# Adaptive-norm transformer block on one core: cosine product on VectorE from PSUM, second key and query projections at other places, 768-key tile transposed through VectorE and DMAs

## What is computed

```python
# x (2, 1024, 256), 16 heads of 128, all float32
h = layernorm(x) * (1 + ca) + sa                 # sa, ca, ... = silu(c) @ wmod
q = (h @ Wq + bq) * 128 ** -0.5;  k = h @ Wk + bk;  v = h @ Wv + bv      # per head
q, k = [t * cos(pos) + rotate_half(t) * sin(pos) for t in (q, k)]        # along the head's 128 columns
attn = softmax(causal(q @ k.T));  x = x + ga * ((attn @ v) @ Wo + bo)
h = layernorm(x) * (1 + cb) + sb
x = x + gb * ffn(h)                              # silu(gate) * up, down; 704 wide, integer weights
```

## Time and profile before

| | |
|---|---|
| median of 3 runs | 1030.65 us (1030.63 to 1032.5) |
| profiled execution, own time | 1031.39 us |
| its span | 1029.6 us |
| busy: TensorE matmuls | 970.8 us, 94% |
| VectorE | 784.1 us, 76% |
| ScalarE | 669.5 us, 65% |
| GpSimd | 764.7 us, 74% |
| DMA engines, mean | 39.2% |

### The profile page before, as it was taken

The page is one execution under the profiler, slowest core; times in us unless marked ns, Lnnn a source line. Parts: engine busy times, 40 slices in busy tenths (PEclk is TensorE's granted clock), DMA queues, the critical chain, the costliest instruction groups (busy, mean ns, idle before and its releaser), DMA issues.

```text
span 1029.6 us, 19698 instructions
## 1 busy us (share of the span) xinstructions
PE 970.8 (94%) x5853; PEld 854.3 (83%) x5853; DVE 784.1 (76%) x1605; ACT 669.5 (65%) x1385; POOL 764.7 (74%) x532
## 2 busy tenths in 40 slices
PE   6988999999999999999999999999999999998897
PEld 5877888888888888888888888888888788887787
DVE  6857877777788788877787778877887777877644
ACT  5756656676666666666666666666666567767763
POOL 3487877788778877787778878787778777885653
PEclk9999999999999999999999999999999999999999
DMA  7524443343334433443434333543344335431011
GB/s 248 166 79 139 118 118 101 107 131 114 102 101 139 127 113 111 138 127 100 115 97 141 103 111 97 148 127 107 107 142 124 109 99 159 139 103 42 1 42 42
DMA packets 86597, 116.74 MB, mean 113 GB/s; under 512 B 10468, under 2 KB 61732, under 8 KB 86564
## 3 DMA queue, kind: packets, MB, share of 16 engines
q1 hardware_dynamic: 86564, 116.33, 39.2%
HBM read 50.17 MB, written 32.57 MB: 80 GB/s over the span
## 4 chain that ended last, share of the span: by engine, by line
PE 62%; POOL 11%; issue 7%; DMA 7%; ACT 6%; DVE 4%; SPq 2%; ACTq 0%; POOLq 0%; DVEq 0%
PE ps_r L1504 13%; PE ps_r L1503 13%; PE ps_r L1502 13%; PE ps_s L1502 5%; PE ps_s L1504 4%; PE ps_s L1503 4%; PE ps_t L1663 4%; POOL swapped L734 3%; DMA swapped<-straight 3%; POOL qk_lo L744 3%; POOL straight L735 2%; DMA side_out<-squares 2%; DMA side_p<-side_out 2%; ACT straight L885 2%; ACT probs L1014 1%
## 5 line engine op out<-in xcount | busy, mean ns | idle before, releaser
L734 POOL TENSOR_TENSOR swapped<-swapped,sin_sb 128x512 f32<-128x512 f32 x124 | 167.5, 1351 | 135.5 <-DMA swapped<-straight 135.0
L1014 ACT ACTIVATE probs<-ps_s,neg_max 128x128 f32<-128x128 f32 (+7 forms) x256 | 190.2, 743 | 109.3 <-DVE neg_max L1394 109.3
L1394 DVE CUSTOM_DVE_ANT_0 ps_s<-ps_s,mask_wide 128x128 f32<-128x128 f32 (+7 forms) x256 | 193.4, 755 | 31.1 <-PE ps_s L1504 29.4
L744 POOL TENSOR_TENSOR qk_lo<-straight,qk_hi 128x512 fp32r<-128x512 f32 x124 | 161.8, 1315 | 63.3 <-ACT qk_hi L898 63.2
L1314 DVE TENSOR_TENSOR pT_lo<-ps_t,pT_hi 128x512 fp32r<-128x512 f32 (+3 forms) x260 | 126.7, 498 | 75.7 <-ACT pT_hi L992 75.6
L735 POOL TENSOR_TENSOR straight<-straight,cos_sb 128x512 f32<-128x512 f32 x124 | 181.8, 1466 | 0.0
L1235 DVE TENSOR_TENSOR straight<-straight,swapped 128x512 f32<-128x512 f32 x126 | 147.1, 1168 | 15.2 <-POOL straight L735 14.7
L754 POOL TENSOR_TENSOR pT_lo<-side_p,pT_hi 128x1024 fp32r<-128x1024 f32 (+1 forms) x62 | 150.9, 2434 | 0.0
L1502 PE MATMUL ps_s<-qk_hi 128*128 128x512 f32 (+4 forms) x384 | 139.8, 364 | 9.7 <-POOL qk_lo L744 9.5
L992 ACT ACTIVATE pT_hi<-ps_t 128x512 fp32r<-128x512 f32 (+3 forms) x260 | 117.1, 450 | 43.0 <-PE ps_t L1663 41.3
L1353 DVE SCALAR_TENSOR_TENSOR y<-ps_r,inv_sum,y 128x256 f32<-128x256 f32 x248 | 108.4, 479 | 35.7 <-PE ps_r L1504 31.7
(11 more groups left out here) (201 smaller groups left out, 2391.0 us busy)
## 6 DMA issues: line engine op xcount, KB each, us to landing
swapped<-straight SPq DMA_DIRECT2D x252, 128.0 KB, 2.3
side_out<-squares SPq DMA_DIRECT2D x31, 512.0 KB, 2.6
side_p<-side_out SPq DMA_DIRECT2D x124, 128.0 KB, 3.0
side_out<-squares SPq DMA_DIRECT2D x31, 448.0 KB, 2.5
side_p<-side_out SPq DMA_DIRECT2D x124, 112.0 KB, 2.5
x_in<-in_L_attn_x SPq DMA_DIRECT2D x4, 512.0 KB, 5.5
w_raw<-in_L_attn_Wk SPq DMA_DIRECT2D x8, 256.0 KB, 3.2
w_raw<-in_L_attn_Wq SPq DMA_DIRECT2D x8, 256.0 KB, 3.8
```

The source lines that it names most:

```text
L734: pool.tensor_tensor(swapped[:, q, :], swapped[:, q, :], sin_sb[:, cs], ALU.mult)
L744: pool.tensor_tensor(lo, rope_buffers(piece)[0][:, RANK[piece] % 2, :], hi.bitcast(F32), ALU.subtract)\
L1014: nc.scalar.activation(halved(t, probs[:, P_AT[step] * P:(P_AT[step] + t + 1) * P]), score_rows(step, t), ACT.Exp, bias=neg_max[:, t:t + 1 ...
L1394: nc.vector.tensor_tensor_reduce(rows, rows, halved(t, mask_wide[:, SEQ - n_keys:SEQ]), -1.0, -MASKED, ALU.add, ALU.min, accum_out=neg_max ...
```

## The change

Three things. (1) The cosine product leaves GpSimd: VectorE reads the piece from PSUM, adds the bias and multiplies by the cosine into `qk_cos` (`cos`), and GpSimd adds `qk_cos` to the swapped copy in place of VectorE. GpSimd so keeps two operations in a `rotate`. The query scale moves into the weights, whose low part VectorE now makes (`wq_low`). `straight` is free again once it is swapped; `swapped` is held until the low part of the piece before in it is made, and the wait for that is on SyncE. A PSUM bank with a projection is free once `cos` has read it. (2) K1 and Q1 are projected ahead of P1. (3) Tile 5 (768 keys, step 5) becomes a side tile; its high and low parts come in the next unit's strings (`side:5-`).

```diff
-SIDE = (7, 6)
+SIDE = (7, 6, 5)
...
 TENSOR_PLAN = """make:K0+ make:Q0+ scores:0 turn:6.0- turn:7.0- scores:1 scores:2 turn:7.1- make:P0- turn:0.0
-        make:P1- scores:3 make:W00- make:K1+ scores:4 make:W01- turn:2.0 make:Q1+
-        make:W10- scores:5 make:W11- make:V0 turn:4.0 scores:6 make:V1 turn:5.0 scores:7
-        turn:5.1"""
-SCALAR_PLAN = """out:K0+ exp:7- turn:6.0- exp:0 split:V out:Q0+ turn:7.0- turn:7.1- high:P0- turn:0.0 exp:1 exp:2
-        high:P1- high:K0+ high:Q0+ exp:3 out:K1+ split:K turn:2.0 exp:4 out:Q1+
-        split:Q side:1 exp:5 turn:4.0 high:V0 high:K1+ high:V1 turn:5.0 exp:6 split:O side:3 turn:5.1 high:Q1+"""
-VECTOR_PLAN = """max:0 turn:6.0- turn:7.0- turn:7.1- max:1 low:P0- add:K0+ max:2 side:1 turn:0.0 add:Q0+ low:P1- max:3
-        sum:W00- max:4 sum:W01- turn:2.0 sum:W10- side:3 max:5 sum:W11- add:K1+
-        turn:4.0 max:6 low:V0 add:Q1+ low:V1 max:7 turn:5.0 turn:5.1"""
-POOL_PLAN = """rotate:K0+ split:V rotate:Q0+ low:K0+ low:Q0+ rotate:K1+ split:K rotate:Q1+ split:Q low:K1+ side:1 low:Q1+
+        make:K1+ scores:3 make:Q1+ scores:4 make:P1- make:W00- turn:2.0 scores:5 make:W01- make:W10- turn:4.0
+        scores:6 make:W11- make:V0 scores:7 make:V1"""
+SCALAR_PLAN = """out:K0+ exp:7- out:Q0+ turn:6.0- exp:0 side:5- turn:7.0- turn:7.1- split:V exp:1 exp:2 high:P0- turn:0.0
+        high:K0+ out:K1+ high:Q0+ out:Q1+ exp:3 split:K exp:4 split:Q high:K1+ high:P1- turn:2.0 high:Q1+
+        side:1 exp:5 turn:4.0 exp:6 high:V0 side:3 split:O high:V1"""
+VECTOR_PLAN = """cos:K0+ cos:Q0+ max:0 turn:6.0- max:1 turn:7.0- max:2 turn:7.1- low:P0- side:1 turn:0.0 cos:K1+ max:3
+        cos:Q1+ max:4 side:3 low:P1- sum:W00- turn:2.0 max:5 split:Q sum:W01- sum:W10- turn:4.0 sum:W11- max:6 side:5 low:V0
+        max:7 low:V1"""
+POOL_PLAN = """rotate:K0+ side:5- rotate:Q0+ low:K0+ low:Q0+ split:V rotate:K1+ rotate:Q1+ split:K low:K1+ low:Q1+ side:1
         side:3 split:O"""
-SYNC_PLAN = """swap:K0+ swap:Q0+ side:1 back:1 swap:K1+ swap:Q1+ side:3 back:3"""
+SYNC_PLAN = """swap:K0+ swap:Q0+ side:1 swap:K1+ swap:Q1+ back:1 side:3 back:3 side:5 back:5"""
...
                 sp.wait_ge(straight_ready, ps.rank(piece, 1))
+                if RANK[piece] >= 6:
+                    sp.nop(nofuse=True)
+                    sp.wait_ge(qk_ready, ps.rank(piece, -1))
...
-                q, chunk = RANK[piece] % 2, piece[3]
-                pool.wait_ge(swapped_ready[q], ps.count((RANK[piece] - 4) // 2 * 32 + 32, PER_PASS["qk"] // 2 * 32))
-                cs = slice(chunk * CH, chunk * CH + CH)
-                pool.tensor_tensor(swapped[:, q, :], swapped[:, q, :], sin_sb[:, cs], ALU.mult)
-                pool.tensor_tensor(straight[:, q, :], straight[:, q, :], cos_sb[:, cs], ALU.mult).then_inc(rotated, 1)
+                _, unit, which, chunk = piece
+                q = RANK[piece] % 2
+                pool.wait_ge(swapped_ready[q], ps.swaps(piece))
+                at_ = slice(chunk * CH, chunk * CH + CH)
+                pool.tensor_tensor(swapped[:, q, :], swapped[:, q, :], sin_sb[:, at_], ALU.mult).then_inc(rotated, 1)
+                pool.wait_ge(cos_ready, ps.cosines(piece))
+                pool.wait_ge(rotated, ps.rank(piece, 1))
+                pool.tensor_tensor(swapped[:, q, :], swapped[:, q, :], qk_cos[:, unit % 2, which, at_], ALU.add).then_inc(qk_sum, 1)
 
             def qk_low(ps, piece):
                 _, unit, which, chunk = piece
-                if piece == ("qk", 1, 1, 0):
-
-                    pool.wait_ge(mod_ready, 2)
                 pool.wait_ge(qk_hi_ready, ps.rank(piece, 1))
                 hi, lo = qk_at(unit % 2, which, chunk * CH, CH)
-                pool.tensor_tensor(lo, rope_buffers(piece)[0][:, RANK[piece] % 2, :], hi.bitcast(F32), ALU.subtract)\
-                    .then_inc(qk_ready, 1)
+                pool.tensor_tensor(lo, swapped[:, RANK[piece] % 2, :], hi.bitcast(F32), ALU.subtract).then_inc(qk_ready, 1)
...
-                nc.scalar.activation(hi, raw, ACT.Copy).then_inc(w_hi_ready[j], 1)
+                nc.scalar.activation(hi, raw, ACT.Copy, scale=SCALE if j == WQ else 1.0).then_inc(w_hi_ready[j], 1)
...
-                if RANK[piece] >= 4:
+                if RANK[piece] >= 6:
+                    act.wait_ge(swapped_ready[q], ps.swaps(piece, 2))
+                elif RANK[piece] >= 4:
                     act.wait_ge(qk_ready, ps.rank(piece, -1))
...
+            def wq_low(n):
+                raw, hi, lo = w_buffers[WQ]
+                dve.wait_ge(w_hi_ready[WQ], n + 1)
+                nc.vector.scalar_tensor_tensor(lo, raw, SCALE, hi.bitcast(F32), ALU.mult, ALU.subtract).then_inc(w_ready[WQ], 1)
...
+            def qk_cosine(ps, piece):
+                _, unit, which, chunk = piece
+                if unit == 1:
+                    dve.wait_ge(mod_ready, 2)
+                dve.wait_ge(straight_ready, ps.rank(piece, 1))
+                dve.nop(nofuse=True)
+                head = ps.count(unit // UNITS * 2 + unit % 2, 2)
+                bias = (bq_s if which == 0 else cols[:, COL_BK:COL_BK + HEADS])[:, bass.ds(head, 1)]
+                at_ = slice(chunk * CH, chunk * CH + CH)
+                nc.vector.scalar_tensor_tensor(qk_cos[:, unit % 2, which, at_], ps_r[:, ps.bank(piece), :], bias, cos_sb[:, at_],
+                                               ALU.add, ALU.mult).then_inc(cos_ready, 1)
...
-                for w, other in ((u, 7), (u - 1, 5), (u - 1, t)) if t == 5 else ((u - 1, 5), (u - 1, t)):
-                    if w >= 0 and other in SIDE and SIDE_SLOT[other] == SIDE_SLOT[t]:
-                        dve.wait_ge(side_ready[other], ps.units_done(w))
-                        break
+                if u > 0:
+                    dve.wait_ge(side_ready[t], ps.units_done(u - 1))
...
-                    pe.wait_ge(straight_ready, ps.rank(old, 1))
+                    if old in FIRST_QK:
+                        pe.wait_ge(straight_ready, ps.rank(old, 1))
+                    else:
+                        pe.wait_ge(cos_ready, ps.cosines(old))
```

70 lines of the change are left out of this document (39 added, 31 removed).

## The result

The changed kernel takes 1230.07 us (median of 4 runs, 1225.1 to 1234.5) where the kernel before, run beside it, takes 1030.64: ratio 1.1931, 95% interval 1.1882 to 1.1981, slower by 19.3%. The forecast was 1108 us with a range of 1030 to 1145. The direction was right, but the time lies outside the range: the loss is 2.6 times the predicted one (+199 us for +77). The profiled execution is the longest of the four (1234.5 us, its span 1232.7).

The account below looks back on a forecast made before the run. TensorE bounds the kernel before; after the change a ring of waits through SyncE, GpSimd and VectorE makes a unit 30.85 us against 28.07, so 28 laps of 2.8 add 78 to 1031.4: 1108 us, range 1030 to 1145.

Parts of the forecast that it names:

- The two paths to P1's low part: One through tile 7's reads and tile 6's squares, one through K1's swap and ScalarE; W01 waits 2 to 2.5 us.
- the second path: K1's swap waits for K0's low part, P1's high part for K1's rotation: 18.3 us, W01 waiting 1 us and more.
- (c): SyncE: K0's swap of the next unit behind tile 5's reads, from its issue to the sine product, 2.9 us.
- (d): GpSimd: rotation of K0, tile 5's low part, rotation of Q0, low parts of K0 and Q0, together 9.35 us.
- (e): SyncE: Q1's swap waits for Q0's low part because it reuses the buffer; its issue takes 1.1 us.
- (g): VectorE: squares of tile 6 after tile 7 has landed, 1.05 us, then P1's low part, 0.65 us.
- (a): Write of tile 5's squares to DRAM, from squares ready to the first read issued, 2.5 us.
- (b): SyncE: issue of the four reads of tile 5, 1.75 us.
- (h): VectorE: work from P1's low part to tile 5's squares (W sums, reciprocals, turns, maxima, squares), 7.1 us.
- the ring: Closed chain of waits through SyncE's queue, GpSimd and VectorE that sets a unit's length: 30.2 us, 30.85 with weight loads.
- (f): Tile 7's reads behind Q1's swap: issues 1.75 us and landing 2.05 us after the last issue, 3.8 together.
- Rival D: Worse: additional 384 KB each way stretch landings by 0.5 us at each of four, 1164 us; chance 0.06.

Follow-up runs that it names:

- four products in the wait: Changed kernel plus four matmuls of 512 columns, read by nobody, on TensorE where it waits for P1's low part: 1221.9 us.
- the run with tile 5 by turns: Changed kernel with tile 5 transposed by TensorE again, no squares, DRAM or reads for it; cosine product and new places kept: 1125.8 us.
- the old queue order alone: Changed kernel with only SyncE's queue changed, tile 7's reads ahead of the swaps of K1 and Q1: 1224.9 us.
- the changed wait alone: Changed kernel where VectorE's squares of a side tile wait until the tile before is written to DRAM, not until it has come back: 1173.2 us.
- the last two versions: Changed kernel, squares waiting for the write alone, ScalarE and VectorE reordered, weight loads earlier: 1058.3 us; then also weight splits, unit 0 and integer weights' loads moved: 1064.4 us.
- four single edits: Changed kernel with one edit each: squares' wait 1173.2 us, SyncE's queue 1224.9, P1's high part earlier on ScalarE 1227.8, tile 6's squares later on VectorE 1300.4.
- the right combination of places: Changed kernel, squares waiting for the write alone, P1's high part ahead of K1's, other ScalarE high parts and VectorE's tile 5 squares moved: 1067.6 us.
- the kernel before with tile 5 (changed wait): Kernel before with tile 5 alone as third side tile, squares waiting for the write of the tile before, not its return: 1200.1 us.

## Why the prediction missed

- **Place and kind of the wait: right.** W01 waits for P1's low part, VectorE stands ahead of the squares of tile 6 until tile 7 has landed, TensorE is busy 86% in the middle (predicted about 85). The two paths to P1's low part were both in the prediction, and the runs show both: taking away one gave 57 us or next to nothing, both 91. With the second path alone W01 waited 3 us; the prediction had "1 us and more".
- **Steps (c), (d), (e), (g), (a), (b): right** to 0.3 us in unit 16, and the cosine form at 0.75 us (measured 0.75). In the mean of the 27 laps (c) is 0.8 us too short, by the laps with weight loads.
- **Step (h) was mis-sized: 8.5 for 7.1 us in unit 16, 8.1 in the mean.** It was built from durations at full clock, and in the four units in which four products in the wait kept the clock up it was 6.9. In the changed kernel TensorE ran at 0.50 behind its own wait, so that VectorE waited 1.4 us for W11's product. That a wait is followed by the lower clock, and so lengthens the ring that made the wait, was in no step.
- **Step (f): 4.75 for 3.8 us, and nearly so in every lap.** The reads took 1.92 to issue behind the swaps and landed 2.7 us after the last. Rival D, landings stretched by the additional transfers, is not the reason: the median read of tile 7 lands 2.9 us after its issue, 3.0 before.
- **A missing step:** 0.9 us between tile 5's reads and K0's swap in unit 16, because ScalarE's copy of K0's projection came 1.3 us behind the projection, after 1.88 us of idle time for which the profile names no releaser. It is so at the end of every fourth unit, where the program's loop starts again (0.6 to 1.0 us in six laps); in the laps into units 4, 8, 12 and so on the copy follows the projection by 0.2 us and the swap the last read by 0.2. That the loop's restart is the reason is argued and not shown. A second closing of the ring, through TensorE, shows in the run with tile 5 by turns, where SyncE has time to spare and the unit is still 31.0 us.
- **"Starting part, unit 31 and the ending keep their length": right for unit 31 and the ending, wrong for units 0, 29 and 30**, +35 us. In unit 0 VectorE waited 7.5 us for tile 7's reads, which stood behind the swaps of K1 and Q1, and TensorE 7.0 for a cosine behind them. The unit took 44.4 us; with the old queue order alone 38.9, with the changed wait alone 39.4, with both 32.9. In unit 29 the integer weights' loads stand ahead of K0's swap; moved behind it they brought the unit from 34.2 to 28.0 us in the last two versions. Unit 31 and the ending grew by 2 us.
- **Weight loads 0.65 us a unit: measured 0.8.** Units with loads took 36.6 us, the others 33.5. I had counted the issues; K0's swap also landed 3.9 us after the end of its issue in such a unit, 1.8 in unit 16.
- **"These gains are worth nothing by themselves": true of the time that VectorE sheds, but the edit has a price that the sum had at nothing.** The cosine out of PSUM is a loss of 67 us alone. I had priced VectorE's time for it, and not what TensorE then waits for; which of the new waits costs how much is in part open.
- The sum: 28 x 2.8 = 78 became 28 x 6.0 = 167 us, plus 35. What the two mis-sized steps and the missing one explain is 3.3 of the 3.5 us by which unit 16's ring exceeds the forecast. In the mean lap, 34.2 us for 30.85 with the loads, (h) and (f) give 1.0 each, (c) and the stretch from the last read to K0's swap 1.9 together, of which the prediction's 0.65 for the loads is to be taken off.
- The prediction's remark of four DMA round trips in the ring counts one too many: its steps wait for three, in (a), (c) and (f).

## What to carry to other kernels

When a step is put behind another on an in-order queue, list every path that ends at the instruction that the bound engine waits for, and ask of each what it would give if the others were gone: here four single edits gave 57, 5, 2 and -70 us, and the right combination of places 163. A semaphore that stands for more than the buffer needs (back in SBUF, where written to DRAM is enough) costs nothing while there is slack and becomes the ring's link when the order is tightened. Handing a PSUM bank's last read to another engine that is itself in a chain of waits can have a price on TensorE, even where that engine's own time goes down: here the edit with its orders cost 67 us, of which the bank itself is a part not measured.

## What the runs showed of the hardware

**VectorE with two fp32 inputs in SBUF beside GpSimd.** The same operation of 128x512 took 0.66 to 2.83 us. VectorE and GpSimd in the kernel before with tile 5 (changed wait):

```profile
601.26 0.65 DVE L1241 TENSOR_TENSOR v_lo<-ps_r,v_hi 128x512 fp32r<-128x512 f32 x1
601.84 2.83 DVE L1235 TENSOR_TENSOR straight<-straight,swapped 128x512 f32<-128x512 f32 x1
604.59 0.68 DVE L1241 TENSOR_TENSOR v_lo<-ps_r,v_hi 128x512 fp32r<-128x512 f32 x1
```

```profile
601.73 2.39 POOL L754 TENSOR_TENSOR pT_lo<-side_p,pT_hi 128x1024 fp32r<-128x1024 f32 x1
```

The addition that began 0.1 us behind GpSimd's ended 0.55 us after it, at 604.67; the subtractions with one operand in PSUM took 0.64 to 0.69 us in all 128 places of this run, 69 of them wholly beside a GpSimd operation. So I read the 1168 ns that the additions removed by the change took in the mean as the cost of their neighbour; the shortest of them took 0.66. The Trainium skill, "SBUF — State Buffer", SBUF: two separate sides, has the two engines share one pair of ports as an exclusive lock, held for the whole instruction, which a VectorE operation with two SBUF inputs needs. This trace agrees: the addition took 2.83 us beside GpSimd's and ended behind it.

**DMA issues on SyncE that stall.** Issues that mostly take 0.3 to 0.6 us took over 0.8 us, up to 1.9, in 15 of 717 places with 34 more instructions a unit on TensorE, in 1 with four more and in 1 to 8 in the others (up to 2.1). The cause was not looked for.

**The clock.** A stand of 3.3 us was followed by about 6 us at the 1.2 GHz level in unit 16; a stand of 2.6 us behind four short products was not followed by any. In unit 20 of that same run a stand of 2.5 us was followed by the lower level, and in the run with the changed wait alone stands of 2.0 us (units 12 and 16) were, while with tile 5 by turns stands of 1.2 to 1.5 us were not. These rows give no threshold.
